# A fused attention, router and expert-FFN kernel on one core: the router's load and the first two token tiles put in another order, no sums over zeros, x's sums in another order, the second quad's copy ahead

## The chip, the cores and the metric

The kernel runs on 1 core of one Trainium2 chip. The metric is the device time of one execution in microseconds (us). Before the change it is 2000.14 us, the median of 3 runs (1999.53 to 2000.66). Engines: PE (TensorE), DVE (VectorE), ACT (ScalarE), POOL (GpSimd), SP (SyncE, which only issues DMAs here).

## The reference, cut to what matters

```python
xn = layernorm(x)                              # x is (4, 1024, 1024): 4096 tokens
# attention branch
q, k, v = xn @ Wq.T + bq, xn @ Wk.T + bk, xn @ Wv.T + bv
kv_sum = cumsum((elu(k) + 1) * v, axis=1)      # over the 1024 tokens of a sequence
s = ((elu(q) + 1) * kv_sum * 64 ** -0.5) @ Wo.T + bo
# FFN branch: 8 experts that share w1, w2; top 2 of a token, 256 slots each
probs = softmax(xn @ router_w.T); top_p, top_i = top_k(probs, 2)
pos = cumsum(onehot(top_i)) - 1; keep = pos < 256
h = gelu(buf @ w1.T + b1) @ w2.T + b2          # buf holds the kept tokens
g = silu(sum over the two choices of h * top_p where kept)
out = x + s * g
```

A token that no expert keeps has g = 0, so its output is x. At most 8 * 256 = 2048 of the 4096 tokens are kept; the kernel computes q, the context, both FFN products and the output projection for these alone, and k, v and the running sums for all tokens.

## The kernel before, in words

There is no scheduler: each engine has its program written out in order, and engines meet at counting semaphores (`wait_ge`, `then_inc`). An engine that waits holds everything behind it.

**Router.** x comes transposed in 8 blocks of 512 tokens (2 MB each), in two buffers that SP refills when PE has read them (L510). PE starts with 11 matmuls on zeros (L1921), then multiplies each block by the router's weights (L1893, 8 chunks of 128 features, fp32, two records a matmul). ACT copies the scores (L922), PE transposes them (L1906, `scores_by_token`), DVE picks the top two (L1331 to L1345). Behind these blocks the 16 chunks of the k and v weights are loaded and split into a high and a low f16 part, the high one on ACT (L911), the low one on DVE (L1321, `low_wkv`). A product of two split operands takes three f16 passes. The router's own 32 KB are loaded first of all by SP (L502) into a tile whose rows have 9 columns per chunk, so that a piece of 8 columns is 32 bytes.

**Tables.** When all tokens have their choices, PE counts them (L1968, L1969), DVE turns the counts into places, drops what is over the capacity (L1365 to L1381), PE ranks the kept tokens (L1975, L1976), and DVE makes the selection columns of the first two tiles (`kept_columns`, L1399), the start of each tile's kept tokens (L1405 to L1412), the number of loop passes (L1409 to L1424, `tables_ready` 1) and the tail (L1428 to L1437, `tables_ready` 2). Then the tables' place in `xnT` is free.

**Token tiles.** 32 tiles of 128 tokens. For each, PE projects k and v in four quarters (L1955, 8 chunks of 3 matmuls each, `project_chunks`), transposes the next tile's normed x and gathers its kept columns in the same matmuls (L1984, `select_x`, in four steps s; ACT reads out steps 0 and 2, DVE steps 1 and 3, L915 and L496/L497), and makes the running sum of k*v of the tile before by a triangular matrix (L2006, `sum_kv`, read by `sums`, L1451, into a window that SP stores). Before tile 0 that sum is made over zeros. Tiles 0 and 1 are written out apart, then a loop takes two tiles per pass. POOL meanwhile adds weight blocks for Strassen's products (L796 to L812) and keeps them in DRAM.

**x's sums.** After the last tile PE makes 32 sums of blocks of the gathered x (L2085, matmuls with an identity), in the order X_ORDER; ACT takes the high part (L1017), DVE the low one (L1548). Sums 4 and 5 are written to the PSUM pair that the last `sum_kv` uses. SP saves parts of the gathered x first (L627), then the last window (L635), then loads the fourth weight block into `spare` (L573).

**Quads.** The rest is 40 quads of 7 products (L2116) with 20 groups of down products (L2145). In a quad ACT copies partial results out of PSUM (L1044): `keep_p1`, `keep_p16`, `keep_p165`, one before each further product into the same bank.

## Time and profile before

| | |
|---|---|
| median of 3 runs | 2000.14 us (1999.53 to 2000.66) |
| profiled execution | 2000.25 us, of which the span from the first to the last instruction is 1998.0 us |
| PE busy | 1970.9 us (99%) |
| DVE, ACT, POOL busy | 1378.4 (69%), 707.4 (35%), 504.6 us (25%) |
| mean granted clock of PE | 0.997 |
| chain that ended last | PE 92%, DVE 3%, DMA 2%, issue 1%, ACT 1% |

The table is read so: PE works nearly all the time, and the time outside the span is 2.25 us. Busy time of PE is the union of its matmuls, whose ends are modelled: 24 matmuls of 128x512 that follow each other start 0.216 us apart, but each is shown with 0.379 us, so a gap between two groups is up to 0.17 us longer than the idle time printed.

### The profile page before, as it was taken

Reading aid. Unit: us, or ns where it says so; the run is one execution under the profiler, and the core shown is the slowest. Engines: PE = TensorE matmul, PEld = TensorE weight load, DVE = VectorE, ACT = ScalarE, POOL = GpSimd, SP = SyncE. Lnnn points to the kernel's source line nnn. Section 1 sums busy time; section 2 is a strip of 40 time slices with the busy share of each in tenths; the row PEclk is TensorE's granted clock in tenths of the full one; section 3 lists DMA queues with packets and bytes.
Section 4 is the critical chain, followed back from the end, with each engine's and each line's share of the span. In section 5 each row is a group of like instructions: output and inputs, shape, how many; then the busy total and the mean of one; then the engine's idle time right before and its main releaser. Section 6 shows DMA issues by size and latency. Waiting matters only on the chain.

```text
span 1998.0 us, 27184 instructions
## 1 busy us (share of the span) xinstructions
PE 1970.9 (99%) x9393; PEld 902.9 (45%) x9393; DVE 1378.4 (69%) x2101; ACT 707.4 (35%) x1112; POOL 504.6 (25%) x640
## 2 busy tenths in 40 slices
PE   9999999999999999999999999999999999999996
PEld 2455554455444444444444444444444444444442
DVE  4887878887877777776777797564455565456656
ACT  1432223222754344344335443522212322322322
POOL 0048888888312321321310010210000000000002
PEclk9999999999999999999999999999999999999998
DMA  9546667667999988978777879673333233335535
GB/s 388 203 141 221 228 228 236 227 212 205 304 331 286 254 243 268 281 235 279 251 263 236 293 257 324 201 222 101 102 104 101 90 114 102 111 106 159 183 114 129
DMA packets 182203, 416.26 MB, mean 208 GB/s; under 512 B 18592, under 2 KB 71376, under 8 KB 179664
## 3 DMA queue, kind: packets, MB, share of 16 engines
q1 hardware_dynamic: 138736, 284.26, 43.4%
q0 software_dynamic: 34896, 121.71, 20.0%
q10 hardware_dynamic: 8464, 8.92, 1.5%
q8 instruction: 60, 0.98, 0.2%
q14 instruction: 47, 0.39, 0.1%
HBM read 268.51 MB, written 163.10 MB: 216 GB/s over the span
## 4 chain that ended last, share of the span: by engine, by line
PE 92%; DVE 3%; DMA 2%; issue 1%; ACT 1%; SPq 0%; DVEq 0%; POOL 0%; ACTq 0%; POOLq 0%
PE pair L2145 36%; PE pair L2116 34%; PE pair L1955 16%; PE pair L1893 3%; PE pair L1984 1%; DMA arena<-up_sums 1%; PE pair L2006 1%; DMA spare<-up_sums 0%; PE pair L1906 0%; DMA arena<-x_t 0%; DVE arena L1548 0%; PE pair L2085 0%; DVE arena L1321 0%; DVE root L1300 0%; DVE arena L1315 0%
## 5 line engine op out<-in xcount | busy, mean ns | idle before, releaser
L2145 PE MATMUL pair<-arena 128*128 128x512 f16 x3360 | 730.2, 379 | 1.1 <-DVE arena L1694 0.5
L2116 PE MATMUL pair<-xnT,arena 128*128 128x512 f16 x2400 | 525.4, 379 | 2.1 <-ACT xnT L1044 1.9
L2145 PEld LDWEIGHTS pair<-arena 128*128 128x128 f16 x3360 | 327.8, 98 | 400.2 <-issue 7.2
L1686 DVE SCALAR_TENSOR_TENSOR arena<-pair,arena 128x1024 f32<-128x1024 f32 x234 | 286.0, 1223 | 150.7 <-PE pair L2145 149.8
L1955 PE MATMUL pair<-arena 128*128 128x512 f16 x1728 | 382.9, 379 | 1.7 <-DVE xnT L497 1.0
L1118 ACT ACTIVATE arena<-arena 128x512 f16<-128x512 f32 x280 | 171.4, 626 | 554.8 <-PE pair L2145 500.0
L2116 PEld LDWEIGHTS pair<-xnT,arena 128*128 128x128 f16 x2400 | 234.4, 98 | 286.6 <-ACT xnT L1044 3.4
L1955 PEld LDWEIGHTS pair<-arena 128*128 128x128 f16 x1728 | 168.6, 98 | 194.1 <-issue 1.9
L2116 PE MATMUL pair<-xnT 128*128 128x512 f16 x960 | 213.7, 379 | 0.0
L1661 DVE SCALAR_TENSOR_TENSOR arena<-arena 128x512 f16<-128x512 f32 x280 | 189.3, 688 | 16.4 <-ACT arena L1118 15.7
L839 POOL DMA_DIRECT2D s_dram<-arena x8 | 6.2, 776 | 596.4 <-DVE arena L1686 596.4
L1044 ACT ACTIVATE xnT<-pair 128x512 f32<-128x512 f32 x120 | 71.2, 594 | 220.2 <-PE pair L2116 220.1
L2116 PEld LDWEIGHTS pair<-xnT 128*128 128x128 f16 x960 | 93.9, 98 | 113.3
L858 POOL DMA_INDIRECT meta_dram<-meta,slot_i x32 | 33.5, 1048 | 367.0 <-PE pair L2145 304.7
L1567 DVE SCALAR_TENSOR_TENSOR arena<-arena 128x1024 f16<-128x1024 f32 x70 | 85.5, 1223 | 27.6 <-ACT arena L1037 27.1
L1105 ACT ACTIVATE arena<-arena,b_c 128x512 f32<-128x512 f32 x96 | 69.2, 721 | 74.7 <-DVE arena L1597 39.1
L972 ACT ACTIVATE arena<-arena 128x512 f32<-128x512 f32 x36 | 22.7, 629 | 162.4 <-DVE arena L1465 162.4
L1604 DVE TENSOR_TENSOR arena<-xnT,pair 128x512 f32<-128x512 f32 x40 | 27.4, 686 | 74.2 <-PE pair L2116 74.0
L1561 DVE SCALAR_TENSOR_TENSOR arena<-arena 128x512 f16<-128x512 f32 x82 | 59.0, 720 | 21.5 <-ACT arena L1026 20.0
L1037 ACT ACTIVATE arena<-arena 128x1024 f16<-128x1024 f32 x70 | 72.8, 1043 | 0.0
L1608 DVE TENSOR_TENSOR arena<-xnT,pair 128x512 f32<-128x512 f32 x40 | 27.5, 687 | 62.7 <-ACT xnT L1044 62.7
L1597 DVE TENSOR_TENSOR arena<-xnT,pair 128x512 f32<-128x512 f32 x40 | 27.4, 685 | 54.4 <-PE pair L2116 53.9
(217 smaller groups left out, 1817.5 us busy)
## 6 DMA issues: line engine op xcount, KB each, us to landing
down_dram<-arena SPq DMA_DIRECT2D x70, 512.0 KB, 7.0
arena<-down_dram SPq DMA_DIRECT2D x70, 512.0 KB, 3.3
up_dram<-arena SPq DMA_DIRECT2D x90, 256.0 KB, 6.0
arena<-up_dram SPq DMA_DIRECT2D x90, 256.0 KB, 2.6
arena<-down_sums SPq DMA_DIRECT2D x40, 512.0 KB, 6.1
arena<-w_up POOLq DMA_DIRECT2D x36, 512.0 KB
up_sums<-arena POOLq DMA_DIRECT2D x36, 512.0 KB, 3.8
arena<-up_sums SPq DMA_DIRECT2D x66, 256.0 KB, 6.1
```

Of the source, the lines that this page charges most:

```text
L1037: nc.scalar.activation(down_ring[:, j, :, HI, :], down_stage[d % DS].rearrange("p (c n) -> p c n", c=2), ACT.Copy, scale=WM).then_inc(down ...
L1044: nc.scalar.activation(dst, in_rows(src), ACT.Copy).then_inc(copy_ready, 1)
L1105: nc.scalar.activation(g_block(name), src, ACT.Gelu, bias=b1_c[:, col:col + 1], scale=INV_XM)\
L1118: nc.scalar.activation(g_ops[:, A_NAMES.index(name), k % 2, HI, :], g_block(name), ACT.Copy, scale=CS if is_attention(n) else HS).then_inc ...
L1561: nc.vector.scalar_tensor_tensor(up_ring(j)[:, LO, :], up_stage[a % US], WM, up_ring(j)[:, HI, :], ALU.mult, ALU.subtract).then_inc(up_w[j ...
L1567: nc.vector.scalar_tensor_tensor(down_ring[:, j, :, LO, :], down_stage[d % DS].rearrange("p (c n) -> p c n", c=2), WM, down_ring[:, j, :, ...
L1661: nc.vector.scalar_tensor_tensor(to[:, LO, :], g_block(name), CS if is_attention(k // 2) else HS, to[:, HI, :], ALU.mult, ALU.subtract).th ...
L1686: ins = nc.vector.scalar_tensor_tensor(to, src, scale, to, ALU.mult, ALU.add)
L1893: ins = mm(scores(u), rw_f[:, c, :], xt_in[u][:, c, :], start=(c == 0), stop=(c == CH - 1))
L1955: ins = mm(out_bank(n), xT[u][:, a, c, :], wkv[:, (n // 2) * CH + c, b, e], start=(c == 0 and i == 0), stop=(c == CH - 1 and i == 2), skip ...
L2116: ins = mm(out_to, w[:, a, c * P:(c + 1) * P], x_in_op[:, b, c, :], start=(first and i == 0), stop=(i == 11), skip_group_check=True)
L2145: ins = mm(down_banks(j, t // 2)[:, (t % 2) * BLOCK:(t % 2 + 1) * BLOCK], g_ops[:, A_NAMES.index(DOWN_A[j]), c, a, t * P:(t + 1) * P], dow ...
```

## The change

1. The router's weights are loaded by ACT's queue, contiguously (64 columns, 256 bytes per row), into `rw_in`; DVE copies them into the tile with 9 columns. SP's first DMA is now the first of x.
2. PE starts with 8 matmuls on zeros in place of 11.
3. Of the last block's work, one chunk of tile 0's first projection (3 matmuls) stands ahead of `scores_by_token`.
4. The low parts of weight chunks 14 and 15 are made after `kept_ready` on DVE (WKV_LAST); PE waits for them before the last two chunks of the third quarter.
5. The sum over zeros goes: no `sum_kv` and no `sums` for tile 0. POOL clears the zero source and window 0 (DVE's memset goes), and the `select_x` steps of tile 1 move up.
6. DVE makes both tiles' selection columns one after the other, and what still reads the tables (`prob`, `logits`) before a new, earlier `tables_ready` 1. ACT's copy of tile 0's kept columns waits for that one. Reads of step 1 and 3 by DVE stand ahead of the reads of k.
7. X_ORDER: sum 11 stands behind 4 and 5. DVE does 4 low parts ahead of the last `sums` in place of 6; the last `sums` has no carry and no memset behind it, and its own semaphore count releases PE and SP. `scale_weights` is behind sum 15.
8. In quad 1, `keep_p16` stands directly behind the first `value`.

```diff
+            act.dma_start(rw_in, router).then_inc(router_loaded, 16)
-            sp.dma_start(rw_f[:, :, 0:EXPERTS], router).then_inc(router_loaded, 16)
...
+            nc.vector.tensor_copy(rw_f[:, :, 0:EXPERTS], rw_in).then_inc(zeros_ready, 1)
...
-        X_ORDER = (0, 1, 2, 3, 6, 7, 8, 9, 10, 11, 4, 5, 14, 15, 12, 13) + tuple(range(16, 32))
+        X_ORDER = (0, 1, 2, 3, 6, 7, 8, 9, 10, 4, 5, 11, 14, 15, 12, 13) + tuple(range(16, 32))
...
+            pool.wait_ge(scores_done, TOKEN_BLOCKS)
+            nc.gpsimd.memset(kv_hl[:, :, :], 0.0).then_inc(kvlo_ready, 2)
+            pool.wait_ge(wkv_ready, 12)
+            nc.gpsimd.memset(window[0], 0.0).then_inc(win_ready, 1)
...
-            nc.vector.memset(kv_hl[:, :, :], 0.0).then_inc(kvlo_ready, 2)
+            for q in WKV_LAST:
+                low_wkv(q)
...
-            kept_columns(0, 0).then_inc(select_ready, 1)
+            for u in range(2):
+                kept_columns(u, u).then_inc(select_ready, 1)
...
-            for _ in range(11):
+            for _ in range(8):
                 mm(out_bank(2), zeros[:, 0:P], zeros, start=True, stop=True)
...
-            project_chunks(0, 0, range(CH)).then_inc(proj_done, 1)
+            project_chunks(0, 0, range(1))
+            scores_by_token(1, TOKEN_BLOCKS - 1)
+            project_chunks(0, 0, range(1, CH)).then_inc(proj_done, 1)
...
             project_chunks(0, 3, range(0, 3))
             pe.wait_ge(stage_act, 2)
-            pe.wait_ge(kvlo_ready, 2)
-            sum_kv(0, 1, 4)
+            pe.wait_ge(select_ready, 2)
             pe.wait_ge(kxlo_ready, 2)
             select_x(1, 0, 3)
+            select_x(1, 1, 2)
             project_chunks(0, 3, range(3, 5))
-            pe.wait_ge(stage_dve, 3)
-            select_x(1, 1, 2)
-            project_chunks(0, 3, range(5, 7))
             pe.wait_ge(stage_act, 3)
             select_x(1, 2, 3)
+            project_chunks(0, 3, range(5, 6))
...
-            for i in X_ORDER[:6]:
+            for i in X_ORDER[:4]:
                 low_x_sum(i)
-            sums(0, last, 10 * pairs + 4)
...
-            nc.vector.memset(scratch[31], 0.0).then_inc(sums_done, 1)
+            sums(0, last, 10 * pairs + 4, last=True)
...
                 value(k, 0)
+                if k == 1:
+                    keep_p16(k)
                 if ups:
                     high_up(k + 1, 1)
-                if not before and not finishing:
+                if k != 1 and not before and not finishing:
                     keep_p16(k)
```

Three places show how this stands in the engines' rows. The first is PE from the last chunks of the router's scores to tile 1's first projection; before:

```order
L1893 MATMUL pair<-arena,rw_f 9x512 x2
L1906 MATMUL pair<-xnT 128x9 x4
L1955 MATMUL pair<-arena 128x512 x24
...
L1993 MATMUL pair<-spare,arena 128x128 x16
L1955 MATMUL pair<-arena 128x512 x9
L2006 MATMUL pair<-spare,arena 128x128 x16
L1984 MATMUL pair<-spare,arena 128x256 x4
L1955 MATMUL pair<-arena 128x512 x6
L1984 MATMUL pair<-spare,arena 128x256 x4
L1955 MATMUL pair<-arena 128x512 x6
L1984 MATMUL pair<-spare,arena 128x256 x8
L1955 MATMUL pair<-arena 128x512 x51
```

And the same place of PE in the changed kernel:

```order
L1918 MATMUL pair<-arena,rw_f 9x512 x2
L1979 MATMUL pair<-arena 128x512 x3
L1931 MATMUL pair<-xnT 128x9 x4
L1979 MATMUL pair<-arena 128x512 x21
...
L2022 MATMUL pair<-spare,arena 128x128 x16
L1979 MATMUL pair<-arena 128x512 x9
L2013 MATMUL pair<-spare,arena 128x256 x8
L1979 MATMUL pair<-arena 128x512 x6
L2013 MATMUL pair<-spare,arena 128x256 x4
L1979 MATMUL pair<-arena 128x512 x3
L2013 MATMUL pair<-spare,arena 128x256 x4
L1979 MATMUL pair<-arena 128x512 x54
```

Three projection matmuls moved ahead of the transposed scores, the 16 of the sum over zeros are gone, and between the selection steps stand 6 and 3 projection matmuls where 6 and 6 stood. The second place is DVE from the last weight chunks to the selection columns; before:

```order
L1321 SCALAR_TENSOR_TENSOR arena<-arena 128x1024 x4
L1365 COPY xnT<-pair 128x512
...
L1381 CAST kept_h<-routing 128x32
L1382 MEMSET arena 128x1024
L1385 TENSOR_TENSOR routing<-xnT 128x32 x2
L1386 TENSOR_TENSOR routing<-routing,xnT 128x256
L1391 COPY routing<-pair 128x32
...
L1399 TENSOR_SCALAR spare<-spare,rank_kept 128x128
L1405 SCALAR_TENSOR_TENSOR routing<-xnT,routing 128x32
```

And the same place of DVE in the changed kernel:

```order
L1342 SCALAR_TENSOR_TENSOR arena<-arena 128x1024 x2
L1386 COPY xnT<-pair 128x512
...
L1402 CAST kept_h<-routing 128x32
L1342 SCALAR_TENSOR_TENSOR arena<-arena 128x1024 x2
L1407 COPY routing<-pair 128x32
...
L1415 TENSOR_SCALAR spare<-spare,rank_kept 128x128 x2
L1422 SCALAR_TENSOR_TENSOR routing<-xnT,routing 128x32
L1424 TENSOR_TENSOR routing<-xnT 128x32 x2
L1426 TENSOR_TENSOR routing<-routing,xnT 128x256
```

Two of the four low parts moved behind the first chain, the memset left DVE, and the three small operations on `prob` and `logits` moved behind the columns. The third place is ACT at the start of quad 1 (L1118 splits the last operands of quad 0, L1105 is `value`, L1044 the copies, L1026 the split of the next weights); before:

```order
L1044 ACTIVATE xnT<-pair 128x8x64
L1118 ACTIVATE arena<-arena 128x512 x4
L1026 ACTIVATE arena<-arena 128x512
L1105 ACTIVATE arena<-arena,b_c 128x512
L1026 ACTIVATE arena<-spare 128x512
L1044 ACTIVATE xnT<-pair 128x8x64
```

And the same place of ACT in the changed kernel:

```order
L1061 ACTIVATE xnT<-pair 128x8x64
L1135 ACTIVATE arena<-arena 128x512 x4
L1043 ACTIVATE arena<-arena 128x512
L1122 ACTIVATE arena<-arena,b_c 128x512
L1061 ACTIVATE xnT<-pair 128x8x64
L1043 ACTIVATE arena<-spare 128x512
```

The copy and the split of the block in `spare` have changed places, in this quad alone.

## Rows read from the trace of the kernel before

**Rows 1.** the page: busy time of each engine, its share, its instructions

```profile
PE 1970.9 (99%) x9393; PEld 902.9 (45%) x9393; DVE 1378.4 (69%) x2101; ACT 707.4 (35%) x1112; POOL 504.6 (25%) x640
```

**Rows 2.** PE's waits over the span: us in total, times, longest us

```profile
PE pair L2116 <- ACT xnT L1044: 1.9, 3, 1.1
PE pair L1955 <- DVE xnT L497: 1.0, 2, 0.6
```

**Rows 3.** timeline of the start: start us, us, engine, line, [idle before]

```profile
0.80 0.68 SPq L502 DMA_DIRECT2D rw_f<-router  x1
1.26 4.40 PE L1921 MATMUL pair<-arena 128*128 128x512 f16 x11 [1.26 <-DVE arena L1263]
1.54 0.63 SPq L517 DMA_DIRECT2D arena<-x_t  x1
10.20 5.32 PE L1893 MATMUL pair<-arena,rw_f 128*9 128x512 f32 x12 [0.65 <-DMA arena<-x_t]
```

**Rows 4.** DMAs that read x_t in the first 3 us

```profile
DMA to landing us min/median/max: 4.0/5.0/7.5
```

**Rows 5.** 20 to 40 us: busy by engine, PEclk, DMA share, GB/s

```profile
20.00:40.00 20.00, 20.00 (x64) 5.91 (x61) 12.57 (x65) 4.44 (x6) 0.00 (x0) 1.00 1.02 417
```

**Rows 6.** timeline from the last scores to tile 1's first projection

```profile
70.57 0.59 ACT L922 ACTIVATE xnT<-pair 9x512 f32<-9x512 f32 x1 [0.32 <-PE pair L1893]
71.21 1.05 PE L1906 MATMUL pair<-xnT 9*128 9x9 f32 x8 [0.68 <-ACT xnT L922]
74.49 4.62 DVE L1321 SCALAR_TENSOR_TENSOR arena<-arena 128x1024 f16<-128x1024 f32 x4
79.03 0.68 DVE L1365 COPY xnT<-pair 128x512 f32<-128x512 f32 x1
85.78 0.18 DVE L1381 CAST kept_h<-routing 128x32 f16<-128x32 f32 x1
87.44 0.18 DVE L1391 COPY routing<-pair 128x32 f32<-128x32 f32 x1
90.29 1.94 ACT L915 ACTIVATE xnT<-pair 128x1024 f16<-128x1024 f32 x2 [15.35 <-DVE routing L1424]
91.75 0.18 DVE L1437 CAST slot_i<-routing 128x32 int32<-128x32 f32 x1
92.28 1.07 PE L2006 MATMUL pair<-spare,arena 128*128 128x128 f16 x16 [0.62 <-ACT xnT L915]
92.75 0.69 DVE L1465 SCALAR_TENSOR_TENSOR arena<-pair,arena 128x512 f32<-128x512 f32 x1 [0.82 <-issue]
98.33 0.68 DVE L497 CAST xnT<-pair 128x512 f32 x1
99.11 1.24 PE L1955 MATMUL pair<-arena 128*128 128x512 f16 x5 [0.78 <-ACT xnT L915]
```

**Rows 7.** timeline of x's sums and of quads 0 and 1

```profile
506.89 0.60 PE L2085 MATMUL pair<-xnT,ident 128*128 128x512 f16 x2 [0.54 <-DVE routing L1556]
508.51 7.40 SPq L573 DMA_DIRECT2D spare<-up_sums  x1
510.34 0.61 PE L2085 MATMUL pair<-xnT,ident 128*128 128x512 f16 x2 [0.25 <-DVE arena L1548]
523.88 0.63 ACT L1026 ACTIVATE arena<-spare 128x512 f16<-128x512 f32 x1 [2.12 <-DMA spare<-up_sums]
529.25 7.94 PE L2116 MATMUL pair<-xnT,arena 128*128 128x512 f16 x36 [0.18 <-ACT xnT L1044]
553.04 0.61 ACT L1026 ACTIVATE arena<-spare 128x512 f16<-128x512 f32 x1
553.56 0.58 ACT L1044 ACTIVATE xnT<-pair 128x512 f32<-128x512 f32 x1
554.19 2.76 PE L2116 MATMUL pair<-xnT,arena 128*128 128x512 f16 x12 [1.15 <-ACT xnT L1044]
```

**Rows 8.** DMAs that write xraw_dram, issued from 499.4 to 502.0 us

```profile
DMA to landing us min/median/max: 8.1/12.4/17.4
```

More of the change, by code:

```diff
@@ L964, in zero_columns, with tile @@
                 act.wait_ge(x_filled, 1)
-            def tile(t, u, first=False, second=False):
+            def tile(t, u, start=None, first=False, second=False):
                 def exp_k(half):
@@ L976, in tile @@
                     exp_k(0)
-                at = act.value_load(start_i[0:1, ds(t + 2, 1)], min_val=0, max_val=SLOTS)
-                for s in range(4) if second else (0, 2):
+                if first:
+                    act.wait_ge(stage_done, 8)
+                    apart(act)
+                    read_selected(copy, 1, 2, 3, ds(start, P), stage_act)
+                else:
+                    at = act.value_load(start_i[0:1, ds(t + 2, 1)], min_val=0, max_val=SLOTS)
+                for s in () if first else range(4) if second else (0, 2):
                     act.wait_ge(stage_done, 5 * t + 4 + 1 + s + 1)
@@ L1004, in tile @@
                     high_x()
-            tile(0, 0, first=True)
+            tile(0, 0, at, first=True)
             tile(1, 1, second=True)
+            pairs = act.value_load(loops_i[0:1, 0:1], min_val=2, max_val=TILES // 2)
             with act.Fori(1, pairs) as g:
```

100 lines of the change are left out of this document (57 added, 43 removed).

## The prediction

> **What bounds the kernel now.** I read the page first: PE is busy for 1970.9 of 1998.0 us [rows 1]. So the change can bring only what PE stands idle, 27 us with the tail behind the last matmul, plus the PE work that it takes away. Then PE's own waits [rows 2] and the timelines around them [rows 3, 6, 7]. The reader should see that the waits are few and lie in three places: the start, the tables with tiles 0 and 1 (60 to 99 us), and x's sums with quads 0 and 1 (505 to 554 us). Between them, in the tile loop, PE waits only twice for DVE's copies, 1.0 us in all [rows 2]; what PE gains at 99 us therefore arrives at 500. I count in arrival times of PE, since printed waits are up to 0.17 us short where matmul ends are modelled.
>
> **The start (parts 1 and 2).** PE's 11 matmuls on zeros run from 1.26 to 5.66 us, 0.43 apart by the pitch that 4.40 us allow; then come scores until PE waits for the second half of block 0, which it gets at 10.20 us [rows 3]. From there the DMA share is 1.02 at 417 GB/s [rows 5]: x and the weights come at the pace of the DMA engines, and block 1 and 2 are hardly early. What starts the stream decides: x's first DMA is issued at 1.54 us, behind the router's at 0.80 [rows 3]. With the router on ACT's queue it is issued at 0.80, 0.74 us earlier. The first piece landed after 4.0 us, at 5.54 [rows 4], so now at 4.8; 8 zeros end at 1.26 + 8 * 0.43 = 4.7 us. They fit. PE's wait at 10.20 ends at 9.46. The 32-byte pieces of the router become 256-byte pieces; what that gives the stream I bound by 0 and 0.3 us and take 0. Gain 0.74 us, between 0.4 (the two queues share the engines) and 1.0.
>
> The zeros run at half the pace of later f16 matmuls of this shape (0.43 against 1.24 us for 5, of which 0.38 is the last one's shown length, 0.22 each [rows 3, 6]): that is the 1.2 GHz level of PE's clock, before the scores, which run at 2.4. In the changed kernel the first scores start at 4.8 us, when PE before was still at the lower level. If one or two of their records (0.43 us each at 2.4 GHz) run at 1.2, PE comes to the wait at 9.46 still in time: 8 records and the small sum are 3.9 us, so it has 0.8 us to spare, worth almost two slow records. The Trainium skill says the same in "TensorE: Matmul & The Clock Gate", section "What's actually happening": PE starts at the half rate and rises only after having been kept busy. By this rule fewer zeros speak against the change, and the case in which the rise comes late is a rival below.
>
> **The last scores (part 3).** At 71.21 us PE has waited 0.68 us for ACT's copy of the last scores (70.57 to 71.16) [rows 6]. Three projection matmuls, 3 * 0.216 = 0.65 us, now fill it; their operands are there by the order of ACT and DVE before. Gain 0.65 us. PE has then 1.39 us in hand. The small matmuls start 0.74 earlier, at 70.47, take 1.0, then come 21 projection matmuls (4.5) and the two that count the choices (0.4): these end near 76.4, in place of 71.21 + 1.0 + 24 * 0.216 + 0.4 = 77.8 us.
>
> **The tables (parts 4 and 6).** DVE could not use that before: four low parts, 4.62 us from 74.49, held L1365 until 79.03 [rows 6]. Two of them go, 2 * 1.155 = 2.31 us, and DVE is free at 76.7, when the counts come. So L1365 starts at 76.7, 2.3 earlier. Its chain to the end of `kept_h` is 79.03 to 85.96, 6.93 us [rows 6]: 83.6. Low parts 14 and 15 then take 2.31: 85.95. PE has done the first quarter's rest, 24 and 12 matmuls (7.8 us) from 76.4, is at the rank matmuls at 84.2 with no wait, does 6 more (1.3), and waits for part 15 from 85.5 to 86.0: 0.5 us that was not there before. Six matmuls more: 87.3. DVE from L1391 to the end of L1437 was 87.44 to 91.93, 4.49 us [rows 6]; the two operations on `prob` and one on `logits` come in (three small ones like L1381, 0.18 each [rows 6], so 0.5 us; 0.2 to 0.8), a small memset goes (0.1). So the columns are ready at 87.0 (no wait for PE) and the tables' last operation ends near 90.85.
>
> ACT's copy of the kept columns (1.94 us) held PE until 92.28, since it waited for `tables_ready` at 90.29 [rows 6]. Now the signal comes about 1 us behind the columns, at 88.0, as PE's columns of the high part do: the copy ends at 90.0. PE arrives there at 87.3 + 16 small matmuls (0.9) + 9 (1.94) = 90.1. The wait of 0.62 us is gone.
>
> **Tile 1's operands (part 5).** The 16 matmuls over zeros (0.9 us of PE) and DVE's reading of them go. PE: 90.1, two selection steps (0.9), 6 matmuls (1.3): 92.3; a step, 3 matmuls, a step: 93.8; 6 matmuls: 95.1. DVE: free at 90.85, plus the 0.82 us without work before L1465 [rows 6], which I keep: 91.7. It copies step 1 (two operations like L497, 0.68 each, 1.3 us): 93.0, in time for PE's step 3 at 93.3; reads k (0.65); and copies step 3, which PE ends at 93.8, by 95.3. Before, the same copy ended at 99.01, and PE went on at 99.11 [rows 6]. So PE starts tile 1's projection at 95.4: gain 3.7 us, of which DVE's copy of step 3 sets the end, 0.3 behind PE's own work. The single gains are in this number and are not added again. The price of an error: everything late on DVE after `kept_h` counts fully from 0.3 us on less; I give 2.6 to 4.0.
>
> Hidden edits: POOL's memsets lie between the last scores and ACT's use of the zeros behind `tables_ready`, some 20 us on an engine with nothing else, so they cost 0; if DVE is slowed by them it is before 74 us, where it has little to wait for, 0 to 0.3 us. DVE's copy of the router ends before the zeros do. The value loads that move behind tile 1 stand where DVE waits for PE.
>
> **x's sums (part 7).** PE waits 0.54 us for the last window and 0.25 for a low part at 506.89 and 510.34 [rows 7], with the hidden gaps about 1.1. With two low parts of some 0.6 us fewer ahead of `sums` and some 0.5 us of carry and memset gone, the signal comes at about 505.2; PE, idle from about 506.3 and now without sum 11's 0.43 us ahead of sum 4, comes there at 505.9. Both waits go. But what is next? ACT splits the block in `spare` only at 523.88, after 2.12 us of idling for its DMA, and from there works without a break until the copy that releases PE at 529.25 [rows 7]. That DMA was issued at 508.51 and its issue alone took 7.40 us [rows 7]: it stands behind the 3 MB saved from 499.4 on, the last of which landed 17.4 us after an issue at 502.0, at 519.4 [rows 8], and behind the window. ACT may not overwrite what is saved (sum 24 on) before 519.4 either. Issued 1.7 us earlier it lands hardly earlier. So PE's 1.1 us are given back as a longer wait before 529.25. I take 0.2 us; the ends are -0.3 and 1.6. The Trainium skill speaks for the low end: "DMA: Bandwidth & Descriptors", section "Queues, rings and completion order", has the descriptors of one ring consumed in ring order, so an earlier issue into a full ring moves nothing; the trace agrees by the 7.40 us of the issue.
>
> **Quad 1 (part 8).** PE waits 1.15 us at 554.19 for the copy that ACT makes at 553.56, behind the split at 553.04 [rows 7]. With the two exchanged the copy starts 0.52 us earlier, and PE still waits. DVE's low part of that split follows it and can come at most 0.6 us later; no product needs it in this quad. Gain 0.5 us, 0.3 to 0.6.
>
> **The sum.** 3.7 + 0.2 + 0.5 = 4.4 us off the profiled execution's 2000.25 us: 1995.8. That execution stands 0.1 us above the median of the runs shown, within their spread, so I leave it there. The tail is not touched.
>
> **The rivals.**
> (a) The gain at x's sums is real: the fourth block lands with the earlier issue, the whole chain of `spare` and PE's 1.1 us with it, and more of the 1.15 us at 554. For it: every link of that chain waits for a DMA. Against it: the full ring. Then 1.3 to 2.0 us more: 1994.1.
> (b) The head brings less: two low parts and three small operations behind `kept_h` make DVE late for the columns and again for step 3, or the start moves less than 0.74. Each 0.5 us on DVE behind `kept_h` is 0.5 us of the end, since cover is 0.3 us. For it: DVE is now the chain almost without a gap from 76.7 to 95.3. With 1.5 us less: 1997.3.
> (c) PE's clock rises late: all 8 records of block 0's first half and the small sum run at 1.2 GHz. PE comes to the second half at 4.8 + 8 * 0.86 + 0.8 = 12.5 in place of 9.46; DMA is then ahead and gives nothing back. 3.0 us of loss: 1998.8. Against it: PE is busy without a gap from 1.26 us, as before. The page named above is the source of this rule.
> (d) Slower: the tile loop. DVE is busy for 69% of the span [rows 1] and works beside POOL there, and in two of some 28 tiles its copy L497 was late, 1.0 us in all [rows 2]. POOL's first units now fall differently against DVE. If every second tile lost 0.5 us, 14 * 0.5 = 7 us go: 2002.8. It decides from 9 late copies on, where 4.4 us are used up. Against it: POOL's start and PE's move together.
>
> **How the numbers follow.** Forecast 0.52, (a) 0.2, (b) 0.18, (c) 0.05, (d) 0.05. What a measurement of this kernel can tell from no change is 0.2%, 4.0 us, here below 1996.1, so the forecast lies just beyond it. Of the forecast's own case (1995.2 to 1996.6) some 70% count as faster, with all of (a) 0.57; (b), (c) and the rest of the forecast are within, 0.39; (d) is slower, 0.04. The range 1993.9 to 1998.2 holds (a) and (b) and leaves out (c), (d) and the outer edges.
>
> **What would show it.** PE's second half of block 0 at about 9.5 us; no wait at the last scores; L1365's successor near 76.7; PE waiting about 0.5 us for the last low part; tile 1's projection at 95.4; the two waits of x's sums gone, but the wait before quad 0's third product grown from 0.2 to about 1.2 us, the block in `spare` still split near the same distance from the loop's end; the wait in quad 1 near 0.6. I am wrong if tile 1 starts later than 96.5, if the wait in quad 0 doesn't grow, or if PE waits in the loop more than a few times.

## The result, and the profile after

The changed kernel takes 1995.51 us in the median (1993.84 to 1999.63, 19 runs), the kernel before 2000.26 us beside it (1998.34 to 2001.91, 19 runs): ratio 0.998, 95% interval 0.9974 to 0.9986, so 2.8 to 5.2 us less. Forecast were 1995.8 us and 1993.9 to 1998.2. The changed kernel's runs reach over 5.8 us, those of before over 3.6; the experiments show one source of that.

PE's busy time in the page and the list of its waits (line waited for, us in total, times, longest), to be set beside [rows 1, 2]:

```profile
PE 1968.6 (99%) x9374; PEld 901.7 (45%) x9374; DVE 1383.1 (69%) x2095; ACT 706.4 (35%) x1112; POOL 508.3 (25%) x642
...
PE pair L2144 <- ACT xnT L1061: 1.7, 2, 1.0
PE pair L1946 <- DVE arena L1283: 1.3, 1, 1.3
PE pair L2173 <- DVE arena L1711: 0.6, 1, 0.6
PE pair L2173 <- DVE arena L1719: 0.5, 2, 0.2
PE pair L2112 <- DVE xnT L499: 0.4, 1, 0.4
PE pair L1918 <- DVE rw_f L1289: 0.4, 1, 0.4
PE pair L1979 <- DVE arena L1342: 0.2, 1, 0.2
```

The waits for ACT at the last scores and in tiles 0 and 1 are gone, and so are both waits in x's sums. What is left of ACT's is the quads' (L2144). New are 0.38 us for the router's copy (L1918) and 0.2 us for a low part (L1979); the wait for DVE at the first x sum (L2112) belongs to the tile loop. The timeline of the start (start, us, engine, line, then the idle time before it and its releaser), for [rows 3]:

```profile
0.81 0.41 ACTq L912 DMA_DIRECT2D xnT<-router  x1
0.81 0.40 SPq L516 DMA_DIRECT2D arena<-x_t  x1
1.26 3.59 PE L1946 MATMUL pair<-arena 128*128 128x512 f16 x8 [1.26 <-DVE arena L1283]
4.98 0.20 DVE L1289 COPY rw_f<-xnT 128x64 f32<-128x64 f32 x1 [3.73 <-DMA xnT<-router]
5.22 3.89 PE L1918 MATMUL pair<-arena,rw_f 128*9 128x512 f32 x8 [0.38 <-DVE rw_f L1289]
9.04 0.39 PE L1956 MATMUL pair<-xnT 128*128 128x8 f32 x2
9.36 3.17 PE L1918 MATMUL pair<-arena,rw_f 128*9 128x512 f32 x7
```

x goes out at 0.81 us, as forecast. But the scores start at 5.22, not at 4.8: they wait for DVE's copy of the router, whose load landed 4.1 us after its issue. This counts in full, because PE no longer waits for the second half of block 0: it goes from the small sum at 9.04 straight on at 9.36, where PE before stood idle for 0.65 us [rows 3]. So in the changed kernel it is PE that sets this time, not the stream of x. The first half is longer too, 3.89 us for its 8 records against 3.59 in the profile of before. Over the eleven profiles with parts 1 and 2 it takes 3.60 us in three and 3.89 to 4.60 in eight, over the three without them 3.59 to 3.64, and in none of the eleven does PE wait for x at 9 us. The longest, from the kernel late10 below:

```profile
5.09 4.60 PE L1918 MATMUL pair<-arena,rw_f 128*9 128x512 f32 x8 [0.24 <-DVE rw_f L1289]
9.62 0.39 PE L1956 MATMUL pair<-xnT 128*128 128x8 f32 x2
9.94 5.32 PE L1918 MATMUL pair<-arena,rw_f 128*9 128x512 f32 x12
```

In that half PE's weight loads, one a record, stand 0.82, 0.85 and 0.62 us apart and then 0.43: the first records ran at the lower level of PE's clock, after 8 matmuls on zeros and some 0.2 us without work. (The granted clock in the profile reads 1.00 from 0 to 5 us even where the zeros run 0.42 us apart, so it can't tell the level here; the spacing does.) The tables and tiles 0 and 1, for [rows 6]:

```profile
76.55 0.69 DVE L1386 COPY xnT<-pair 128x512 f32<-128x512 f32 x1 [0.53 <-PE pair L1995]
83.30 0.18 DVE L1402 CAST kept_h<-routing 128x32 f16<-128x32 f32 x1
83.39 2.35 DVE L1342 SCALAR_TENSOR_TENSOR arena<-arena 128x1024 f16<-128x1024 f32 x2
87.84 1.94 ACT L920 ACTIVATE xnT<-pair 128x1024 f16<-128x1024 f32 x2 [13.73 <-PE pair L2022]
94.44 0.68 DVE L499 CAST xnT<-pair 128x512 f32 x1
```

The chain that finds the kept choices starts at 76.55 us (forecast 76.7) and ends with `kept_h` at 83.5 (83.6); the low parts of 14 and 15 follow it; ACT copies the kept columns from 87.84 (88.0); DVE's copy of step 3 ends at 95.1 (95.3). x's sums and quad 0, for [rows 7]:

```profile
503.11 7.96 SPq L572 DMA_DIRECT2D spare<-up_sums  x1
...
514.93 0.60 ACT L1034 ACTIVATE xnT<-pair 128x512 f16<-128x512 f32 x1 [1.10 <-DMA xraw_dram<-xnT]
516.98 0.74 POOL L793 DMA_DIRECT2D up_sums<-arena  x1 [1.01 <-POOL arena L804]
...
518.07 5.34 PE L2144 MATMUL pair<-xnT,arena 128*128 128x512 f16 x24
519.27 0.63 ACT L1043 ACTIVATE arena<-spare 128x512 f16<-128x512 f32 x1 [2.24 <-DMA spare<-up_sums]
524.44 7.93 PE L2144 MATMUL pair<-xnT,arena 128*128 128x512 f16 x36 [1.02 <-ACT xnT L1061]
...
548.61 2.76 PE L2144 MATMUL pair<-xnT,arena 128*128 128x512 f16 x12 [0.63 <-ACT xnT L1061]
```

Quad 0 starts 5.66 us earlier than before, its third product 4.81: the wait of 0.18 us at 529.25 has become 1.02, because ACT again waits for the block in `spare`, whose issue again takes long (7.96 us, before 7.40). Ahead of that ACT now also waits for a save of the gathered x (`xraw_dram`) to land, 1.10 us, which it didn't in the profile of before. In quad 1, 1.15 us of waiting have become 0.63.

POOL's last scatter is issued at 1979.08 us instead of 1984.82, 5.7 us earlier, but the span ends only 3.6 us earlier: from that issue to the end it is 15.3 us here and 13.2 before. In the other twelve profiles below it is 13.6 to 14.3, once 15.4. Where the end falls within these 2 us is thus no work of the change; what decides it stays open.

### The profile page after: what moved, and what is told of

It is laid out like the page before. It is cut to its first block, busy times and chain, and to the rows that moved or that the text cites. A ratio compares the mean times of both kernels' runs of the same rounds, so it can differ in the third digit from the quotient of the medians.

```text
span 1994.4 us, 27141 instructions
## 1 busy us (share of the span) xinstructions
PE 1968.6 (99%) x9374; PEld 901.7 (45%) x9374; DVE 1383.1 (69%) x2095; ACT 706.4 (35%) x1112; POOL 508.3 (25%) x642
## 3 DMA queue, kind: packets, MB, share of 16 engines
q10 hardware_dynamic: 8608, 8.95, 1.4%
## 4 chain that ended last, share of the span: by engine, by line
PE 74%; POOL 12%; DMA 7%; DVE 3%; issue 2%; ACT 1%; DVEq 0%; ACTq 0%; POOLq 0%; SPq 0%
PE pair L2173 36%; PE pair L2144 35%; DMA arena<-w_up 3%; PE pair L1918 3%; DMA arena<-w_down 2%; POOL arena L799 1%; POOL arena L803 1%; POOL arena L801 1%; POOL arena L787 1%; POOL arena L810 1%; POOL arena L814 1%; POOL arena L804 1%; POOL arena L812 1%; POOL arena L815 1%; POOL up_sums L793 1%
## 5 line engine op out<-in xcount | busy, mean ns | idle before, releaser
L2144 PE MATMUL pair<-xnT,arena 128*128 128x512 f16 x2400 | 525.1, 379 | 1.7 <-ACT xnT L1061 1.7
L1979 PE MATMUL pair<-arena 128*128 128x512 f16 x1728 | 382.8, 379 | 0.3 <-DVE arena L1342 0.2
L2144 PEld LDWEIGHTS pair<-xnT,arena 128*128 128x128 f16 x2400 | 234.4, 98 | 285.8 <-ACT xnT L1061 2.6
L1979 PEld LDWEIGHTS pair<-arena 128*128 128x128 f16 x1728 | 168.6, 98 | 193.1 <-ACT arena L920 0.9
L2144 PE MATMUL pair<-xnT 128*128 128x512 f16 x960 | 213.7, 379 | 0.0
L2144 PEld LDWEIGHTS pair<-xnT 128*128 128x128 f16 x960 | 94.0, 98 | 113.3
```

The lines of the kernel that those rows point to most:

```text
L1979: ins = mm(out_bank(n), xT[u][:, a, c, :], wkv[:, (n // 2) * CH + c, b, e], start=(c == 0 and i == 0), stop=(c == CH - 1 and i == 2), skip ...
L2144: ins = mm(out_to, w[:, a, c * P:(c + 1) * P], x_in_op[:, b, c, :], start=(first and i == 0), stop=(i == 11), skip_group_check=True)
```

## All profiles side by side

PE's landmarks, read from the timelines of all 14 profiles. "Half 0": start of the scores of block 0's second half. "Head": from the start of the last 4 score matmuls to the sum of k*v that tile 1's projection precedes (109.47 us in the profile of before). "First": PE's first x sum. "POOL": issue of its last sum made ahead of the quads, counted from "first". "Way": from "first" to quad 0's third product. "Scatter": POOL's last issue.

| kernel | half 0 | head | first | POOL | way | scatter |
|---|---|---|---|---|---|---|
| before | 10.20 | 40.82 | 497.52 | +28.0 | 31.73 | 1984.82 |
| before, again | 9.96 | 40.82 | 497.26 | +18.4 | 31.69 | 1983.77 |
| after | 9.36 | 37.76 | 492.89 | +24.1 | 31.55 | 1979.08 |
| after, again | 8.95 | 37.76 | 494.15 | +18.9 | 30.76 | 1978.83 |
| after, third | 8.96 | 37.76 | 493.58 | +28.8 | 32.07 | 1980.44 |
| head_only | 9.27 | 37.75 | 492.68 | +33.4 | 34.84 | 1983.40 |
| spare_first | 9.23 | 37.75 | 492.20 | +27.2 | 32.09 | 1978.30 |
| u12_start | 9.84 | 37.76 | 492.82 | +35.7 | 36.07 | 1985.08 |
| u3_scores | 9.47 | 38.67 | 494.04 | +34.3 | 34.68 | 1983.73 |
| u4_low | 9.63 | 38.50 | 493.35 | +34.7 | 35.09 | 1983.23 |
| l6_tables | 9.90 | 38.97 | 494.09 | +28.2 | 33.39 | 1982.82 |
| late10 | 9.94 | 37.77 | 492.95 | +38.7 | 34.19 | 1983.75 |
| late14 | 9.04 | 37.75 | 492.01 | +12.5 | 30.25 | 1977.80 |
| late16 | 9.34 | 37.76 | 493.67 | +0.3 | 30.25 | 1981.94 |

Two things stand out. The head is the same to 0.02 us in all nine profiles of kernels whose head is the changed one, so one profile resolves 0.1 us there, though a kernel's time does not. And the way through x's sums varies by 5.8 us, and is mostly the longer, the later POOL's sums end. Not strictly: the two profiles of before need 31.7 us at +28.0 and at +18.4, l6_tables needs 1.3 us more than the third of after with POOL's last sum at the same time (522.3 and 522.4 us), and the latest end (late10) doesn't have the longest way.

## Experiments on the head

**The two kernels once more.**

> The kernel before, unchanged, profiled a second time. What a second look tells is which times repeat. Theory (waits at the written-out places are set by the program): PE enters tile 1 at 99.1 us, x's sums at 497.5 give or take the loop's waits, and waits 0.6 to 1.2 us at the third product of quad 0 together with the fifth of quad 1. Rival (the waits in the tile loop and at the quads fall anywhere): the loop's two late copies and the 0.60 us at 718 us are elsewhere or gone, while the first 100 us are the same to 0.1 us. The stretch from POOL's last scatter to the end (13.2 us in the first look at before, 15.3 at after) should differ again by 1 us or more if it is no work of the change.

1999.97 us, one run.

> The changed kernel, unchanged, profiled and timed again. By my ledger PE is 3.9 us ahead at tile 1, 0.5 more by quad 1, and what the first look showed beyond it (1.3 us in the tile loop, 0.8 at 718 us, lost 0.6 at 1166 us) is no part of the change: so tile 1 at 95.2 us to 0.1, quad 1's restart 4.4 to 5.6 us ahead of before, and a ratio of 0.998 give or take 0.0007. If the loop's 1.3 us came from the change, both looks have the loop without a wait.

1995.77 us (1993.3 to 1998.74, 11 runs), ratio 0.9979 (0.997 to 0.9988). The head repeats; the tile loop does not: here PE waits three times for DVE in it (0.76, 0.46 and 0.47 us, at 376, 423 and 429 us), in the first profile once, at the first x sum (0.39 us). Counted from the end of the head to "first", the tile loop takes 388.99 us here and 387.31 in the first profile, 1.7 us more; since this head ended 0.4 us earlier, the two "first" are 1.3 us apart. The shortest loop of all 14 profiles is 386.76 us.

**Parts 1 and 2 undone** (the router by SP in rows of 9 columns, 11 zeros).

```diff
+            sp.dma_start(rw_f[:, :, 0:EXPERTS], router).then_inc(router_loaded, 16)
...
-            act.dma_start(rw_in, router).then_inc(router_loaded, 16)
...
-            for _ in range(8):
+            for _ in range(11):
```

> Parts 1 and 2 undone: the router is loaded again by SP in rows of 9 columns ahead of x, with 11 matmuls on zeros; all else as in the changed kernel. My theory (the stream of x starts 0.74 us later, and nothing behind it gives that back): PE gets the second half of block 0 at 10.0 to 10.2 us, where the changed kernel had 9.43 and 8.95 in two profiles, and the last tile of sum_kv's first group (L2036, 105.58 and 105.16 in the changed kernel) starts 0.7 us later, at 105.9 to 106.3. Rival (the stream catches up, DMA being at its limit from 10 us on in both): 10.1 us at the second half, but 105.2 to 105.6 at L2036. Span of this one profile within 1993 to 1996.

The second half is read at 9.84 us, a little below what was expected; the head is unchanged. Over all profiles: 10.00 us in the three without these parts, 9.37 (8.95 to 9.94) in the eleven with them, and at the last scores 68.45 against 67.83. So the start is worth 0.6 us on average. It lasts to the tables, since from the second half of block 0 to the last scores PE takes 58.45 to 58.49 us in all 14 profiles. One profile alone can't show the gain, as the spread is as large: within the series of four profiles that this one belongs to (u12_start, u3_scores, u4_low, l6_tables) it is 0.2 us. The spread is that of the slow first records: from the start of the scores (5.09 to 5.22 us) to the second half it is 3.85 us at the least and 4.85 at the most. Which share of the 0.6 us is the router's and which the zeros' was not tried. That this execution took 2000.54 us comes for the most part from x's sums (way 36.07) and the slower product behind them, shown below.

**Part 3 undone** (no three matmuls ahead of the last scores).

```diff
-            project_chunks(0, 0, range(1))
             scores_by_token(1, TOKEN_BLOCKS - 1)
-            project_chunks(0, 0, range(1, CH)).then_inc(proj_done, 1)
+            project_chunks(0, 0, range(CH)).then_inc(proj_done, 1)
```

> Part 3 undone: the last scores come straight behind the transposes again, with no three projection matmuls ahead. My theory: PE waits 0.65 us for ACT's copy near 70 us, the chain of the choices starts when it does in the changed kernel, so that DVE's chain does not move; PE comes to the last low part 0.65 us later, where it had 0.17 us to wait, so that 0.5 us is lost there and at tile 1: L2036 at 105.7 to 106.1 for 105.2 to 105.6. Rival (DVE is the chain from 76.7 us on, so what PE loses ahead of it costs nothing): L2036 at 105.2 to 105.6. A second rival (the full 0.65 us and the chain later too): 106.2 or more.

The head grows by 0.91 us. PE's timeline:

```profile
70.78 1.02 PE L1931 MATMUL pair<-xnT 9*128 9x9 f32 x8 [0.97 <-ACT xnT L927]
...
77.56 0.69 DVE L1386 COPY xnT<-pair 128x512 f32<-128x512 f32 x1 [1.17 <-PE pair L1994]
```

PE comes 0.65 us later with the counts, the length of the three matmuls, and 0.3 us more: the transposed scores start 0.35 us after ACT's copy ends (70.43), in the kernel before 0.05 us. DVE, idle for 1.17 us in front of the chain instead of 0.53, passes all of it on. So neither the expectation (0.5) nor the first rival (0) held: after the change DVE waits for the counts, not the counts for DVE, and everything ahead of them counts in full.

**Part 4 undone in one point** (low parts 14 and 15 ahead of the chain).

```diff
+            for q in WKV_LAST:
+                low_wkv(q)
             def flat4(a):
...
             nc.vector.tensor_copy(kept_h[:, :], kept).then_inc(kept_ready, 1)
-            for q in WKV_LAST:
-                low_wkv(q)
```

> Part 4 undone in one point: DVE makes the low parts 14 and 15 ahead of the chain that finds the kept choices, not behind it. My theory: the chain starts at 78.3 to 78.6 us in place of 76.1 to 76.6, kept_h is there at 85.1 to 85.4 instead of 82.9 to 83.3, PE waits 1.4 us for it where it had come without a wait at 83.7, the 12 matmuls that hid the low parts come behind that wait, and the columns come as in the changed kernel (86.4 to 86.9), so PE is 1.2 to 1.4 us late from there on: L2036 at 106.4 to 107.0. Rival (DVE has the same work before the columns in either order, and the columns set the time): L2036 at 105.2 to 105.6.

The head grows by 0.74 us, between the theory (1.2) and the rival (0), nearer the theory. The rank matmuls of PE and the end of the third quarter:

```profile
85.47 0.19 PE L2002 MATMUL pair<-kept_h,xnT 128*128 128x32 f16 x1 [0.91 <-DVE kept_h L1405]
85.53 2.75 PE L1980 MATMUL pair<-arena 128*128 128x512 f16 x12
```

PE waits 0.91 us for `kept_h` and then no more for a low part (0.18 less). The wait was put too long by the 0.5 us that DVE idles ahead of the chain in the changed kernel; here low parts fill it.

**Part 6 weakened** (ACT's copy of the kept columns by the second signal).

```diff
-            act.wait_ge(tables_ready, 1)
+            act.wait_ge(tables_ready, 2)
```

> Part 6 weakened: ACT's copy of the kept columns waits for the tables' second signal in place of the first, everything else as in the changed kernel. My theory (PE came to tile 0's selection within 0.2 us of the end of this copy, 90.0 us forecast): the copy starts at 88.6 to 89.1 us instead of 87.4 to 87.8, and PE waits 0.6 to 1.3 us for it at the selection's second step; L2036 at 105.8 to 106.8. Rival (there is slack between the copy and PE): L2036 at 105.2 to 105.6 with no wait.

```profile
89.69 1.94 ACT L920 ACTIVATE xnT<-pair 128x1024 f16<-128x1024 f32 x2 [15.04 <-DVE routing L1444]
...
91.68 1.05 PE L2013 MATMUL pair<-spare,arena 128*128 128x256 f16 x8 [1.04 <-ACT xnT L920]
```

The copy starts 1.3 us later against the last scores, PE waits 1.04 us for it, and the head grows by 1.21 us. There was 0.1 us of slack at most: the signal's place is worth more than any other single edit here. The three edits undone at the head add up to 2.86 of its 3.06 us, but single edits needn't add; part 5 was not run by itself, and what it is worth stays open.

**Parts 7 and 8 undone.**

```diff
-        X_ORDER = (0, 1, 2, 3, 6, 7, 8, 9, 10, 4, 5, 11, 14, 15, 12, 13) + tuple(range(16, 32))
+        X_ORDER = (0, 1, 2, 3, 6, 7, 8, 9, 10, 11, 4, 5, 14, 15, 12, 13) + tuple(range(16, 32))
...
-            for i in X_ORDER[:4]:
+            for i in X_ORDER[:6]:
...
-                if k == 1:
-                    keep_p16(k)
```

> The changed kernel with the order of x's sums, the DVE and SP order around the last window sum, and quad 1's copy put back as before; all of the start, the tables and tiles 0 and 1 as changed. My theory: 3.9 of the gain is here, tile 1 at 95.2 us, the two waits of x's sums back (0.5 and 0.25 us), and PE's restart at quad 0's third product hardly later than in the changed kernel, since ACT waits there for a DMA: total 0.3 to 0.8 us slower than the changed kernel, ratio to before 0.9982. Rival (x's sums carry 1.1 us of gain): 1.6 us slower than the changed kernel, 0.9989.

1996.9 us (1994.91 to 1999.19, 11 runs), ratio 0.9984 (0.9975 to 0.9993): 1.1 us above the changed kernel beside it, and the intervals overlap, so parts 7 and 8 are worth 1.1 us at a guess and aren't shown. Both waits in x's sums are back (0.95 and 0.24 us). 2.88 us more are lost at the third product; POOL's sums ended late in this profile, which is also the slowest of the 11 executions. In quad 1 PE has no wait in it, with `keep_p16` back behind the split: PE comes too late to need it. Part 8 was not undone by itself.

## Experiments on x's sums

**The block in `spare` loaded ahead of the window's store.**

```diff
+            sp.wait_ge(stage_dve, 6 * pairs + 3)
+            load_up_op(US - 1)
...
             sp.dma_start(win_dram[:, :, ds(at, P)], window[0]).then_inc(sums_stored, 16)
-            load_up_op(US - 1)
```

> The changed kernel with two DMAs of SP exchanged: the load of the fourth weight block into spare is issued before the store of the last window (1024 pieces of 512 bytes) in place of behind it. Theory (the block waits in a full ring behind what was issued before it, so its landing and not its issue sets PE's restart): it lands 2 to 4 us earlier, ACT's split of it is no longer late (2.24 us of idling before), PE's wait of 1.02 us at quad 0's third product goes, and of the 0.63 us at quad 1 at least a part: PE is 1.0 to 1.7 us ahead of the changed kernel at quad 1's fifth product. Rival (the load is slow by shared bandwidth with POOL's and SP's other transfers, whatever stands ahead of it): the landing moves less than 1 us and PE's waits stay within 0.3 us. Third possibility: ACT is then held by the landing of the saved x (519.4 us before), and PE gains only some 0.5 us.

1995.28 us (1993.69 to 2000.08), ratio 0.9979 (0.997 to 0.9988), the same as the changed kernel. ACT and PE:

```profile
516.20 0.64 ACT L1043 ACTIVATE arena<-spare 128x512 f16<-128x512 f32 x1
...
520.62 0.63 ACT L1043 ACTIVATE arena<-arena 128x512 f16<-128x512 f32 x1 [2.81 <-DMA arena<-up_sums]
...
524.29 7.94 PE L2144 MATMUL pair<-xnT,arena 128*128 128x512 f16 x36 [1.68 <-ACT xnT L1061]
```

The block is there 3.1 us earlier (2.4 counted from "first"), without a wait, and the next one, loaded into the arena, is late in its place; the way is 32.09 us. So the order of these two is not what binds. The DMA engines are busy for 0.99 of the time from 494 to 526 us in this profile, which suggests that the stretch lacks DMA time whatever the order; the next kernels test that.

**What takes the DMA time.** The four single profiles of the head hinted at it: in all four, whose edits lie 400 us earlier, "way" is 33.4 to 36.1 us instead of 30.8 to 32.1, and POOL's sums end late, as in head_only's (34.84). Why in all four stays open; they ran in one series. POOL makes 76 sums of weight blocks ahead of the quads, each with 0.5 MB in and 0.5 MB out, and 12 late ones in the quads. The next three kernels move that border.

```diff
-        LATE_UNITS = 12
+        LATE_UNITS = 10
```

For 14 and 16, the first 2 and 4 rounds of the quads also take three late sums in place of two (loads at p = 0, 3, 6).

> The changed kernel once more, beside the next three. Over the ten profiles so far PE's way from its first x sum to quad 0's third product is 30.8 to 32.1 us where POOL's last in-time sum is stored by 520 us, and 33.4 to 36.1 us where it is stored at 522 to 528 us. My theory: how early PE comes out of the tile loop is only worth something if POOL's sums of weights are done by then, since their traffic and that of SP share the DMA engines between 495 and 530 us. So this run is near 1995.5 us in the median, 1993.5 to 1999 over its runs, and its profile falls on that line: 31 us with an early store, 34 to 36 us with a late one. Rival (chance in PE's and ACT's order, POOL unrelated): a profile off that line.

1995.80 us (1993.23 to 1999.99, 11 runs), ratio 0.9979 (0.997 to 0.9988). POOL's last sum is issued at 522.4 us, for which 34 to 36 us of way were expected; it is 32.07. The line between the two groups is thus not a sharp one.

> Two more of the weight sums (76 in time in the changed kernel, 12 late) are made in time by POOL, before the quads: 78 in time, 10 late. They bring 2 MB more of traffic and 10 us of POOL into the stretch of x's sums. My theory: POOL's last in-time store is at 523 to 539 us, PE's wait before quad 0's third product (0.4 to 1.0 us in two profiles of the changed kernel) is 3 to 5 us, with the clock's fall behind it, and the median is 1.5 to 4 us above the changed kernel's beside it. Rival (SP's own 3.5 MB set that wait, or the late stretch was past PE's need): the same within 0.7 us.

1999.74 us (1998.33 to 2002.93, 11 runs), ratio 1.0001 (0.9992 to 1.001): the change's whole gain is gone, 3.9 us above the changed kernel beside it, with intervals that don't touch. The wait before the third product is 2.67 us, less than the 3 to 5 expected, and the clock's fall behind it isn't in this profile; but PE also waits 0.95 us before quad 0 and 2.22 in its fifth product. ACT, PE and POOL:

```profile
517.66 0.60 ACT L1034 ACTIVATE xnT<-pair 128x512 f16<-128x512 f32 x1 [3.35 <-DMA xraw_dram<-xnT]
519.13 5.34 PE L2144 MATMUL pair<-xnT,arena 128*128 128x512 f16 x24 [0.95 <-DVE xnT L1572]
521.76 0.63 ACT L1043 ACTIVATE arena<-spare 128x512 f16<-128x512 f32 x1 [2.01 <-DMA spare<-up_sums]
527.14 7.93 PE L2144 MATMUL pair<-xnT,arena 128*128 128x512 f16 x36 [2.67 <-DVE xnT L1572]
...
531.60 0.74 POOL L793 DMA_DIRECT2D up_sums<-arena  x1 [0.30 <-POOL arena L804]
...
545.06 7.94 PE L2144 MATMUL pair<-xnT,arena 128*128 128x512 f16 x36 [2.22 <-ACT arena L1122]
```

PE's two waits are put down to DVE, which works beside POOL here, so a rival is that POOL slows DVE. It doesn't explain them: up to the third product two of DVE's operations of this kind are longer than their 0.68 us (0.99 and 0.88), 0.5 us in all, while ACT, for which DVE waits in turn, stands 7.4 us for DMAs, 5.4 of them for the saves of x and 2.0 for `spare`.

> Two fewer of the weight sums in time: 74, and 14 late. The quads' first two rounds take three late sums each instead of two. My theory: POOL's last in-time store comes 10 us earlier, at 503 to 518 us, PE's wait before quad 0's third product goes (0 to 0.4 us) and PE needs 30.8 to 31.3 us from the first x sum to it; median 1 to 3 us below the changed kernel's beside it. Rival (ACT's wait for the block in spare comes from SP's full queue alone): the wait stays at 0.4 to 2 us and the median within 0.7 us of it. On the other side: POOL's sums in the quads hold DVE, and PE waits there: slower.

1994.88 us (1993.45 to 2000.44, 11 runs), ratio 0.9976 (0.9967 to 0.9985): the lowest median of all, 0.9 us below the changed kernel beside it, which such runs can't tell from nothing; one run still takes 2000.44 us. The mechanism shows in the profile, though:

```profile
515.71 0.63 ACT L1048 ACTIVATE arena<-spare 128x512 f16<-128x512 f32 x1 [0.24 <-DMA spare<-up_sums]
517.08 13.11 PE L2149 MATMUL pair<-xnT,arena 128*128 128x512 f16 x60
...
637.58 2.76 PE L2149 MATMUL pair<-xnT,arena 128*128 128x512 f16 x12 [0.78 <-ACT xnT L1066]
710.93 2.76 PE L2149 MATMUL pair<-xnT,arena 128*128 128x512 f16 x12 [0.66 <-ACT xnT L1066]
```

Quad 0 runs through its third product without a wait. In return PE waits at 637 and 711 us, in the two rounds with a third late sum.

> Four fewer in time: 72, and 16 late, three in each of the quads' first four rounds. My theory: POOL is done 21 us earlier, at 492 to 507 us; what late14 gains is nearly all there is, since x's sums then run with SP's traffic alone; 0 to 1 us below late14. Rival (POOL's memory accesses also slow DVE in the stage): more than 1 us below late14. Slower than late14 if the third late sum in a round comes in the way of DVE's work there.

1996.86 us (1994.91 to 1997.47, 11 runs), ratio 0.9983 (0.9974 to 0.9992): 2.0 us above late14, the last clause of the expectation, though the two intervals overlap. The way is 30.25 us as in late14, so nothing more was to be had there, and four rounds pay 1.10, 0.56, 1.10 and 1.10 us, where late14 pays 0.78 and 0.66: 2.4 us more. The first of them:

```profile
630.39 1.06 POOL L803 TENSOR_TENSOR xnT<-xnT 128x256 f32<-128x256 f32 x1
630.78 1.75 DVE L1594 SCALAR_TENSOR_TENSOR arena<-arena 128x1024 f16<-128x1024 f32 x1
631.41 1.70 POOL L804 TENSOR_TENSOR xnT<-xnT 128x256 f32<-128x256 f32 x1
632.46 1.21 DVE L1588 SCALAR_TENSOR_TENSOR xnT<-arena,xnT 128x512 f16<-128x512 f32 x1
639.42 1.90 PE L2149 MATMUL pair<-xnT,arena 128*128 128x512 f16 x8 [1.10 <-ACT xnT L1066]
```

DVE takes 1.75 and 1.21 us beside POOL for what takes it 1.22 and 0.68 us in the same quad of the changed kernel, and the copy that PE waits for is behind that. The Trainium skill, "SBUF — State Buffer", section "SBUF: two separate sides", says that a VectorE instruction with two SBUF inputs and a GpSimd instruction that reads SBUF lock the ports they share against each other: whichever starts first has them for its whole instruction, and the other blocks. The lengthening by 0.53 us, less than the 0.72 us of such a POOL instruction alone, is compatible with it; no run here tests it.

The share of time of the DMA engines from 494 to 526 us, and what POOL's queue moved in it, complete the row: 0.99 and 5.2 MB (late10), 0.94, 0.91 and 0.94 and 3.6, 3.2 and 4.2 MB (the three of after), 0.83 and 2.1 MB (late14), 0.65 and 0.5 MB (late16). The Trainium skill, "DMA: Bandwidth & Descriptors", section "Issuing engines are not separate DMA queues", has it that DMAs of all issuing engines run on the same 16; these shares agree. The saves of x show what it does to a single transfer: the last of SP's four lands 20.4 us after its issue in late10, 18.2 to 19.5 in the three of after, 16.9 in late14 and 12.5 in late16. Up to the copy that releases the third product, ACT waits for these saves and for the next weight blocks 7.4 us in late10, 3.3 to 4.1 in the three of after, and 0.2 and 0.4 in late14 and late16.

PE's clock adds to some of the long ways. The granted clock from 519 to 560 us is 0.92 in u12_start and 0.96 in u4_low, u3_scores and head_only, else 1.00, and the product behind the wait shows it:

```profile
528.89 10.37 PE L2143 MATMUL pair<-xnT,arena 128*128 128x512 f16 x36 [3.93 <-DVE xnT L1571]
```

10.37 us for 36 matmuls that take 7.93 behind the wait of 2.67 us in late10. Behind the waits of 4.54 (u4_low), 2.88 (head_only) and 2.80 us (u3_scores) they take 9.62, 9.62 and 9.46 us. There PE ran for a while at the lower level of its clock, which costs 1.5 to 2.4 us on top of the way.

## Why the prediction was right, point by point

- **Start.** Forecast 0.74, measured 0.63 on average (0.6 at the last scores). The size came out, the mechanism did not, and that is luck in part. By the forecast PE waits for the second half of block 0 until 9.46, because the stream starts 0.74 us earlier. In none of the eleven profiles does it wait for it: the half was there by 8.95 us, and PE's own arrival sets the time. It starts at 5.09 to 5.22 in place of 4.8, held by the router's copy, and needs 3.60 to 4.60 us for the first 8 records. The 0.8 us to spare, "worth almost two slow records", don't exist, and rival (c) comes true in part: in eight profiles the first records are slow, by up to 1.0 us, on average over all eleven by 0.4.
- **Tables and tile 1.** Forecast, with the start, 3.7 us at tile 1's projection. The head gives 3.06 and the start 0.63: 3.69. In the first profile every landmark (76.7, 83.6, 88.0, 95.3 us) came within 0.2 us. Only the wait for the low parts was forecast at 0.5 us and is 0.2, in every profile in which the low parts lie where the change put them.
- **One size was off inside it.** Part 3 was taken for 0.65 us; undone it costs 0.91. And the head was treated as bound by DVE from `kept_h` on; ahead of it PE's counts are the bound (DVE idles 0.53 us at 76 us). The forecast left the start of DVE's low parts at 74.49 us, where before had it, though everything ahead of them moves with the start: they began at 73.66. So DVE is free at 76.0, not at 76.7, and that the chain starts near 76.7 even so is because PE's counts come at 76.5.
- **x's sums.** That both waits go and come back before the third product is right: forecast about 1.2 us there, measured 1.02, 0.35 and 1.48. The term of 0.2 us came out as well: the way is 31.7 us in both profiles of before and 31.5 on average in the three of after, which are 1.3 us apart. The reason was half right. It is DMA time, but not the full queue in front of `spare`: reordered, the block lands 3 us earlier and PE gains nothing (spare_first). Of what is moved from 494 to 526 us in the first profile, 6.05 MB are SP's and 3.64 POOL's, and POOL's share decides: 2 MB more of it, made ahead of the quads, cost 3.9 us (late10). The landing of the saved x, which the forecast named as a bound for ACT, is the one of ACT's waits that grew most there: 5.4 us for 1.1 to 3.4 in the three of after.
- **Quad 1.** 1.15 and 0.74 us of wait before, 0.63, 0 and 0.63 after: 0.5 us on average, as forecast; no run isolates it.
- **The sum.** 4.4 us forecast, 4.2 to 4.8 between the medians of three series. The third product comes 4.1 us earlier on average (three profiles against two), the last scatter 4.85.
- **The rivals.** (a) comes true only in the executions where POOL ends early (after, again: 0.9 us less way than before), and not by an earlier issue (spare_first); (b) is ruled out by the head's 3.06 us. (c) comes true in part, see the start: not 8 records at the lower level and 3.0 us, but at most the first few and 1.0 us. (d) had the right pair, POOL and DVE, in the wrong place: against the shortest loop of 386.76 us, those of after take 0.55, 2.23 and 1.61 us more and both of before 1.3; but POOL's phase does decide how much of the gain is kept, in x's sums. That would explain why the changed kernel's runs reach from 1993.2 to 2000.0 us, but it isn't shown: no slow execution of it was profiled, and late14, where POOL's sums end early in the one profile, has a run of 2000.44 us too. POOL starts 1.2 us earlier than before (89.7 for 90.9), PE arrives 4 us earlier. This was not priced, and the forecast held because on average it costs little: that is luck.

## What to carry to other kernels

When one engine reaches a stage earlier, ask which other engines' work the stage assumes done, and by how much they come earlier too; here PE gained 4 us on POOL, and two more of POOL's sums were enough to eat all of it. Where a kernel's time is too noisy for a small edit, distances between landmarks of the same engine (the head, 37.76 us in nine profiles) resolve a tenth of a microsecond in one profile. When a wait names one transfer in a stretch with DMA at over 90%, reordering can just move the wait to the next transfer (spare_first); less traffic in the stretch took it away (late14). And when a forecast has an engine arrive ahead of its data, check that every step of that arrival holds: here the engine became the bound, unnoticed, because the size came out.

## What the runs showed of the hardware

- A 32 KB load alone on ACT's queue, issued at 0.81 us together with the first of x on SP's, landed after 4.1 us, as late as the 4.0 us of x's first piece before [rows 4]; in all eleven profiles of kernels that load it so it took 3.9 to 4.1 us. First on SP's queue, ahead of x and in pieces of 32 bytes, it took 3.1 and 2.6 us in the two profiles of before: beside the stream it isn't faster.
- PE that had to wait at the last scores went on 0.3 us later than what it waited for explains (2.86 us from the last scores to the transposed scores, 2.57 without the wait); in the kernel before, which also waited there, that distance is 2.56. What makes the difference stays open.
- Four DVE operations beside POOL's, in the round of late16 shown above, were each 0.53 us longer (one 1.75 for 1.22, three 1.21 for 0.68), whatever their length.
- SP's issue of one 256 KB load took 3.0 to 8.4 us in this stretch and held everything SP had to issue behind it: 3.0 ahead of the window's store (spare_first); behind it 7.0 to 8.3 in the three of after, 8.4 in late10, 5.7 in late14 and 4.3 in late16, where POOL moved less.
- PE's first score records, behind 8 matmuls on zeros and 0.2 to 0.6 us without work, took up to twice their time (0.82 to 0.85 us apart for 0.43, late10) in some executions and not in others of the same kernel; behind 11 zeros they did not in three profiles.
- In the middle of the kernel the granted clock fell behind waits of PE of 2.80, 2.88, 3.93 and 4.54 us, and stayed at 1.00 behind waits of 2.65 and 2.67 us; 36 matmuls took 9.46 to 10.37 us in place of 7.93.
